# Six images through convolution, attention and table first; the last two run beside GpSimd's gathers, with the histogram and two scan stages between

## What is computed

```python
x = relu(sum over 32 paths of conv1x1(conv3x3(conv1x1(x))) + x)   # each with batch norm and relu
t = tokens(x)                                                     # 8 * 3136 = 25088 tokens of 64
t = t + attention(layernorm(t))     # 8 heads, each token sees a 7 x 7 window of its image
t = t + experts(layernorm(t))       # 4 experts, the best 2 mixed
```

## Time and profile before

| what | value |
|---|---|
| median of 3 runs | 5481.44 us (5479.78 to 5503.6) |
| profiled execution | 5501.74 us, span 5500.1 us |
| busy share of the span | PE 48%, PEld 33%, DVE 49%, ACT 27%, POOL 53% |
| stages, start to start | convolution 0 to 1302, attention to 2178, table to 2354, edges to 5233, finish to 5500 |
| within edges | histogram 2354 to 2690, scatters and first four chunks to 3179, then 12 chunks |

### The profile page before, as it was taken

How to read it: one execution, slowest core, us unless ns; L and a number is a source line. 1 busy time by engine, 2 the same in 40 slices (tenths; PEclk the granted TensorE clock), 3 DMA queues, 4 the chain that set the end, 5 groups by cost and what they waited for, 6 DMA issues and landing times. The chain is left out here.

```text
span 5500.1 us, 58955 instructions
## 1 busy us (share of the span) xinstructions
PE 2650.6 (48%) x15808; PEld 1819.7 (33%) x15808; DVE 2685.6 (49%) x4278; ACT 1510.6 (27%) x5776; POOL 2903.6 (53%) x3274
## 2 busy tenths in 40 slices
PE   6888888886999997967600061101111001111023
PEld 2454445544888886845300020000000000000022
DVE  7988878873999997589500051101111101111077
ACT  1333334344888886200000041101111001111000
POOL 1000000001666665367777767777777777777663
PEclk8888888885999998555555575555555555555555
DMA  5766667774666664431111041111111111111154
GB/s 95 106 109 110 106 103 108 114 108 71 100 103 103 102 104 86 107 87 11 24 8 7 2 127 37 37 8 38 38 37 37 23 23 38 36 36 33 9 183 140
DMA packets 592730, 378.76 MB, mean 69 GB/s; under 512 B 404821, under 2 KB 524421, under 8 KB 589861
## 3 DMA queue, kind: packets, MB, share of 16 engines
q1 hardware_dynamic: 388597, 214.70, 17.7%
q10 hardware_dynamic: 94224, 109.47, 11.7%
q0 software_dynamic: 109728, 52.69, 8.7%
HBM read 231.54 MB, written 144.24 MB: 68 GB/s over the span
## 5 line engine op out<-in xcount | busy, mean ns | idle before, releaser
L1599 POOL DMA_INDIRECT e_row<-scratch_table,e_edge x2048 | 1979.0, 966 | 706.5 <-issue 671.3
L1788 PE MATMUL f_psY<-f_hid,f_w 128*64 128x512 f32 x392 | 135.6, 778 | 2206.0 <-ACT f_hid L1733 2206.0
L1684 DVE TENSOR_TENSOR e_e<-e_row,e_b 128x512 f32<-128x512 f32 x16 | 11.1, 697 | 1733.9 <-DMA e_row<-scratch_table,e_edge 1733.6
L1788 PEld LDWEIGHTS f_psY<-f_hid,f_w 128*64 128x64 f32 x392 | 38.4, 163 | 2288.5 <-ACT f_hid L1733 2128.2
L984 POOL MEMSET a_wproj<- 128x128 f32 x1 | 0.2, 209 | 1278.6 <-POOLq L172 1278.6
L1747 ACT ACTIVATE e_weight<-e_drop 128x1024 f32<-128x1024 f32 x16 | 16.9, 1056 | 2164.6 <-DVE e_drop L1697 2164.6
L1097 ACT ACTIVATE prob<-psS,low 128x100 f32<-128x100 f32 x1568 | 512.3, 372 | 62.9 <-DVE low L1130 62.9
L496 PE MATMUL psH<-h,c_w 128*128 128x448 f32 x1008 | 512.4, 596 | 3.8 <-ACT h L602 2.0
L824 DVE SCALAR_TENSOR_TENSOR acc<-psE,acc 128x896 f32<-128x896 f32 x392 | 425.3, 1085 | 94.1 <-PE psE L513 86.4
L1032 PE MATMUL psS<-keys,q_exp 84*128 84x100 f32 x3136 | 390.7, 275 | 38.9 <-DMA keys<-in_kfeat 38.7
L513 PE MATMUL psE<-stack,c_w 75*128 75x448 bf16 x896 | 337.3, 418 | 125.9 <-DVE acc L824 115.5
(11 more groups left out here) (284 smaller groups left out, 5515.2 us busy)
## 6 DMA issues: line engine op xcount, KB each, us to landing
stack<-scratch_parts ACTq DMA_DIRECT2D x504, 112.0 KB
e_row<-scratch_table,e_edge POOLq DMA_INDIRECT x2048
scratch_y<-f_y ACTq DMA_DIRECT2D x49, 512.0 KB, 2.9
scratch_state<-e_state SPq DMA_DIRECT2D x16, 1536.0 KB, 6.2
g_y<-scratch_y SPq DMA_DIRECT2D x24, 1024.0 KB, 6.2
val<-scratch_vpad SPq DMA_DIRECT2D x672, 35.0 KB
scratch_parts<-h2p ACTq DMA_DIRECT2D x56, 336.0 KB, 9.4
keys<-scratch_kpad SPq DMA_DIRECT2D x112, 155.0 KB
```

The source lines that it names most:

```text
L1599: pool.indirect_dma_start(out=row[s][:, f, :], out_offset=None, in_=table_dram, in_offset=bass.IndirectOffsetOnAxis(ap=edge[s][:, 0, f:f + ...
```

## The change

The images are split into six early ones and two late ones (`EARLY = 6`), and each of the first three stages takes a range of images. The program's order is now: convolution, attention and table of the early images; `count_phase` (the histogram, with the gathers of chunks 0 and 1); convolution of the late images (scatters and the gather of chunk 2 on GpSimd); a scan stage for chunks 0 and 1 (gather of chunk 3); attention of the late images (gathers of chunks 4 and 5); a scan stage for chunks 2 and 3 (gather of chunk 6); table of the late images (gather of chunk 7); the edge loop with chunks 8 to 15; finish. In the late stages GpSimd's own work moves: the fills to VectorE, the attention's val rows, loads and stores to SP's queue, the table's squares and scaling to VectorE.

```diff
-SORT_SLOTS = (5, 6, 7, 8, 9, 10, 11, 12, 13)
+SORT_SLOTS = (2, 3, 5, 6, 7, 8, 9, 10, 11, 12, 13)
...
-    conv_phase(nc, io, t1, q, kpad, vpad, ordered)
-    attention_phase(nc, io, t1, q, kpad, vpad, t2)
+    early, late = range(EARLY), range(EARLY, N)
+    conv_phase(nc, io, early, t1, q, kpad, vpad, ordered)
+    attention_phase(nc, io, early, t1, q, kpad, vpad, t2, lasting=lasting)
...
+            edges.count_phase(io, digit, first, ends)
+
+            def place(pool):
+                edges.scatter(pool)
+                edges.gather(pool, 0, 2)
+
+            def two(pool):
+                edges.gather(pool, 1, 0)
+                edges.gather(pool, 1, 1)
+
+            conv_phase(nc, io, late, t1, q, kpad, vpad, beside=place, kept_ident=keep.ident)
+            edges.scan_phase((0, 1), lambda pool: edges.gather(pool, 0, 3))
+            attention_phase(nc, io, late, t1, q, kpad, vpad, t2, beside=two)
+            edges.scan_phase((2, 3), lambda pool: edges.gather(pool, 1, 2))
+            table_phase(nc, io, late, t2, z, table, adst, beside=lambda pool: edges.gather(pool, 1, 3))
+            edges.edge_phase(io, z, y)
```

In attention, SP's program for one strip gets what GpSimd issued (`load_rest`: four val rows; `store`, `load_t1`: two transfers each):

```diff
+                    if beside is not None:
+                        load_rest(sp, n, s, st)
+                        if not (first and k <= 3):
+                            store(sp, st.step(-4))
+                        if not (first and k <= 1):
+                            load_t1(sp, st.step(-2))
```

A scan stage loads what its two chunks need, scans them, stores their states and loads the edges of the chunk that takes the place; the last row of the scan is kept for the next stage:

```diff
+    def scan_phase(self, chunks, beside):
...
+                    sp.wait_ge(self.b_placed, 16 * 129)
+                    for c in chunks:
+                        self.load_b(sp, c, c % 2)
+                    for c in chunks:
+                        self.chunk_out(sp, 0, c, True, False)
```

In the edge loop, `PER = TILES_Z // LEFT` is 49 // 12 = 4 tiles of the expert network for a chunk instead of 3, and the exponentials of a chunk now come ahead of them:

```diff
-                        for q in range(par * PER, (par + 1) * PER):
-                            gelus(turn, q, not last or q < 2 * PER - 1)
-                        exps(turn, par)
+                            self.exps(act, self.FIRST + turn * 2 + par)
+                            for q in range(par * PER, (par + 1) * PER):
+                                gelus(turn, q, not last or q < 2 * PER - 1)
```

More of the change, by code:

```diff
@@ L452, in image @@
                         stores(n, t)
-                        if not last and t % 2 == 0:
-                            blank(n + 1, t // 2)
+                        if not last:
+                            blank(n + 1, t)
+                            if t == TILES - 1:
+                                blank(n + 1, TILES)
                 with sp.Fori(0, N - 1) as n:
@@ L940, in every_span, with load_rest, load_t1, store @@
             span(0)
-            with eng.Fori(1, N // 2) as m:
-                span(m)
+            if N > 2:
+                with eng.Fori(1, N // 2) as m:
+                    span(m)
         with nc.Block() as block:
+            def load_rest(eng, n, s, st):
+                wait(eng, pv_ready, 2 * st.i - 6)
+                eng.sem_inc(passed, 1)
+                for ky in range(SP_ROWS, WIN):
+                    eng.dma_start(val[st.at][ky * WIN:(ky + 1) * WIN], windows(n, s * QROWS + ky)).then_inc(v_rest[st.at], 16)
+            def load_t1(eng, st):
+                wait(eng, t2a_done, st.i - 1)
+                eng.sem_inc(passed, 1)
+                for r in range(2):
+                    eng.dma_start(t1[st.par][:, r], t1_view[st.i, :, :, r]).then_inc(t1_loaded[st.at], 16)
+            def store(eng, st):
+                eng.wait_ge(t2_done, st.i + 1)
+                eng.sem_inc(passed, 1)
+                for r in range(2):
+                    eng.dma_start(t2_view[st.i, :, :, r], t2[st.par][:, r]).then_inc(t2_stored[st.at], 16)
+            def fill(eng):
+                eng.memset(wproj[:], 0.0).then_inc(zeroed, 1)
+                for a in q_exp:
+                    eng.memset(a[:], 0.0).then_inc(zeroed, 1)
             @block.sync
@@ L994, in load_t1 @@
-                def load_t1(st):
-                    wait(pool, t2a_done, st.i - 1)
-                    pool.sem_inc(passed, 1)
-                    for r in range(2):
-                        pool.dma_start(t1[st.par][:, r], t1_view[st.i, :, :, r]).then_inc(t1_loaded[st.at], 16)
-                def store(st):
-                    pool.wait_ge(t2_done, st.i + 1)
-                    pool.sem_inc(passed, 1)
-                    for r in range(2):
-                        pool.dma_start(t2_view[st.i, :, :, r], t2[st.par][:, r]).then_inc(t2_stored[st.at], 16)
+                if beside is not None:
+                    beside(pool)
+                    return
@@ L1121, in _ @@
             def _(dve):
+                if beside is not None:
+                    fill(dve)
                 dve.wait_ge(const_in, 16 * N_CONST)
@@ L1398, in _ @@
                         center(i)
+                    if beside is not None and i < COUNT:
+                        squares(dve, i)
                     if 1 <= i <= COUNT:
                         variance(i - 1)
+                    if beside is not None and 2 <= i:
+                        scale(dve, i - 2)
                     if index is not None and 1 <= i <= index.STEPS:
```

793 lines of the change are left out of this document (437 added, 356 removed).

## The result

The changed kernel takes **5150.2 us** as a median of 4 runs (5145.1 to 5155.7), beside 5487.2 for the kernel before: a ratio of 0.9375, interval 0.9361 to 0.939. The forecast was 5160, its range 5085 to 5260. The profiled execution of the changed kernel took 5155.7 us, its span 5154.1.

A forecast was written before the change was run, and what follows sets the result against it. GpSimd's queue of gathers, 1.302 us each, was taken to bound the second half, with convolution's 1302 us free of gathers. Stages from a histogram start at 1889 summed to 5183; minus 20 for profiled run against median gave 5160, range 5085 to 5260.

The forecast's parts named there:

- rival E: Late convolution and attention: gathers go at busy transfer engines' pace; above 2.07 us each the kernel is slower; chance 0.05.
- Early convolution, -228: Six images with the sort packed into eleven slots instead of nine: 1198 us become 970; bounds -245 and -133.
- a tile needs 11.9 us beside its sort: Early convolution: a full tile's 22.91 us less nine compare halves of 1.22 us; 42 such tiles plus 495 us sort.
- Rival C: Early convolution: packed sort feeds TensorE later, all 42 tiles take 25.35 us, stage saves only 133, total 5255; chance 0.11.
- Early attention and table, -204 and -33: Six images instead of eight: 28 attention strips fewer at 7.29 us, seven table tiles fewer at 4.74 us.
- Late convolution, 385: Two late images: 88 us ahead, 268 for tiles without sort, 29 behind; GpSimd's 351 us hidden, 34 to spare.
- rival B: Late convolution and attention: transfer engines slow the gathers to 1.60 us each, total 5266; chance 0.14.
- Late attention, 350: 256 gathers take 333 to 347 us, SP's queue 321 to 357 (55 start, 28 strips at 9.5 to 10.8).
- rival D: Late attention: VectorE's operations shut out GpSimd, gathers stand still 3.2 us a strip, 90 us, total 5250; chance 0.05.
- The histogram's row: Trace of the kernel before: beside VectorE's 512 two-input operations of 700 ns, gathers cost only 1.27 us; cited against D.
- The waits for scanned chunks, 30 each: Second scan stage and edge loop: first gather waits 30 us for edges loaded only after a chunk is scanned.
- The five expert tiles, +22: End of edge loop: five expert-network tiles instead of one follow the last exponential, four more at 5.53 us.

## Why the prediction was right, point by point

- **What bounds it.** Right: GpSimd's queue, at 1.30 us a gather, from the first scan stage to the edge loop's last gather. (As forecast, the histogram stayed VectorE's, busy for 322.0 of 330.8 us, and the late convolution was set by its own work, with GpSimd idle for 23.7 us behind it.) The edge loop's 1024 took 1334.2 us (1333 forecast). Shifting 69 gathers into its gaps moved the end by what the gaps gave up, 61 us, which shows the bound. No mean is above 1.39 us, so rival E had nothing to stand on.
- **The total.** That 5150.2 lies within 10 us of 5160 is in part luck. The stages came out 27 us below their sum, 21 in the part before the histogram and 10 in the histogram, with the rest 4 above, while the profiled run lay 5.5 us above the median and not 20, which gave back 14.5. Where the 10 us of the histogram went is not shown.
- **Early convolution, -228.** Too little: the stage went from 1302.5 to 1052.4, -250, beyond the bound of -245 (for which the prediction shows no working; its smallest sum, 962, is -236). The step that failed is that a tile needs 11.9 us beside its sort. That counted VectorE's idle time in a full tile (22.91 - 20.72 = 2.2 us of the earlier trace rows) as need. The two new slots filled it, so a full tile stayed near 23.0 and did not go to 25.35. Rival C fell by this. With a twelfth slot a full tile does grow, but VectorE is full there; no run shows TensorE fed late, which was C's mechanism.
- **Early attention and table, -204 and -33.** Measured: 674.6 us for 875.5 (-201) and 141.2 for 175.7 (-34).
- **Late convolution, 385.** 378.5. Its parts, by the first fold at 2285.0 and the last tile's at 2535.3: 86 us ahead, 265 for 14 tiles (250.3 + 14.5), 28 behind, for 88, 268 and 29. Its gathers were hidden, but with 24 us to spare and not 34: their instructions stayed at 0.96 us (249.75 / 259), while two pauses grew by 16 us. What the pauses are is not shown, so they speak neither for rival B nor against it.
- **Late attention, 350.** 355.5, by GpSimd and not, as put there, by both alike, so that the nearness of the two numbers is luck. Of SP's part the pace was right: in mid-stage its queue has no gap, and a pair of strips took 2915.39 - 2895.75 = 19.6 us, 9.8 a strip where 9.5 to 10.8 was forecast. The 55 us of start were too many: without gathers the stage took 306 us, below the 321 that SP was to need at least.

```profile
2895.75 3.26 SPq L1005 DMA_DIRECT2D q_exp<-scratch_q  x8
...
2915.39 3.25 SPq L1005 DMA_DIRECT2D q_exp<-scratch_q  x8
```

- GpSimd's part was the term that was too small: 1.389 us a gather where 1.302 to 1.357 was taken. The cause is rival D, at a third of its price: 26 us held instead of 90. The histogram's row, by which D was given 0.05, was misread: its operations are short, and they run in step with the gathers, so that VectorE's own pairs lose the time. One operation of 1.62 us costs the gathers 0.94 us, more than half its length. The rule of the Trainium skill ("SBUF — State Buffer", section "Who interferes with whom") that a VectorE operation with two inputs in SBUF contends with a GpSimd instruction that reads SBUF agrees with 1.06 against 0.96 us; no run here shows whether it was by its reading that a gather was held. The one-input operation of 0.91 us that held too would fit the same section's other case, the two-port mode; no run here shows in which mode an operation ran.
- **The waits for scanned chunks, 30 each.** The 30 ran from SP's first load to the gather; measured so they are 28.0 and 31.1 us (3138.02 - 3110.05 and 3506.96 - 3475.90). The change of stage before that load makes them 33.0 and 35.4.
- **The five expert tiles, +22.** 22.9 in the changed kernel's profile, 16.6 to 17.7 in seven others and 20.1 by the medians, shown by running them ahead of the last exponential.

## What to carry to other kernels

When one queue sets the end, count its gaps, not its busy share: what moved work took out of the gaps here came off the end, and only the change of stage itself could not be filled. A stretch that an engine spends waiting inside a full tile is free room, so look at busy time against duration before a price is put on one more instruction. Beside GpSimd's indirect transfers, try cutting VectorE's long operations into short ones where VectorE has time; here it gave back 20 us of the 26 in the one stage where it was tried.

## What was not expected

- The multiply of 1.62 us holds GpSimd's gathers for 26 of its 45 us a stage; four pieces of 0.52 us, 51 us in all, hold them for 6. The single gather of 3.37 us of the earlier trace rows, which the prediction gave to rivals B and E, looks like the same thing: it lies beside a two-input multiply of 2.27 us in VectorE's scan of a chunk. In the changed kernel's edge loop the ten gathers of 1.9 to 3.0 us all lie beside that multiply, and together they are some 18 us longer than ten of 0.95. Cutting it into pieces was not tried. The first row is of the kernel before, the others of the changed one:

```profile
3389.91 2.27 DVE L1703 TENSOR_TENSOR e_part<-e_row,e_weight 128x2048 f32<-128x2048 f32 x1
...
3571.54 2.27 DVE L1739 TENSOR_TENSOR e_part<-e_row,e_weight 128x2048 f32<-128x2048 f32 x1
3571.59 3.04 POOL L1559 DMA_INDIRECT e_row<-scratch_table,e_edge  x1 [0.31 <-issue]
```

- GpSimd pauses for some 3.2 us once in about 128 indirect transfers; in the late convolution pauses of 5 to 14 us stood in every profile, though the instructions between were no slower. What the pause is, and why it grows there and not in attention, stays open.
- Between two stages 3 to 12 us pass; leaving out the clearing of semaphores took off 2.4 at most.
